# Routed tiles of a mixture of experts: five passes of TensorE for the second product in place of six, with the last 48 gated columns held twice

## What is computed

```
xn = layernorm(x)
attention: 16 heads of 128, keys and values from a latent of 128, causal softmax
moe:  scores = sigmoid(xn @ gate_w.T);  the two best of 8 experts, weights normalised, times 2.5
      h = einsum('td,edh->eth', xn, w1);  u = einsum('td,edh->eth', xn, w3)      # 176 hidden columns
      y = einsum('eth,ehd->etd', silu(h) * u, w2)
      routed = einsum('etd,te->td', y, combine)
      shared = silu(xn @ sw1) * (xn @ sw3) @ sw2
out = x + attention + routed + shared
```

## Time and profile before

| | before |
|---|---|
| median of 3 executions | 752.09 us |
| profiled execution, its own time | 751.67 us |
| its span, from the first to the last instruction | 749.9 us |
| mean granted clock of TensorE, as a share of full speed | 0.990 |
| busy share of the span: PE, VectorE, ScalarE, GpSimd | 94%, 86%, 78%, 66% |

### The profile page before, as it was taken

The page is one execution under the profiler, slowest core; times in us unless marked ns, Lnnn a source line. Parts: engine busy times, 40 slices in busy tenths (PEclk is TensorE's granted clock), DMA queues, the critical chain, the costliest instruction groups (busy, mean ns, idle before and its releaser), DMA issues.

```text
span 749.9 us, 15632 instructions
## 1 busy us (share of the span) xinstructions
PE 704.7 (94%) x4554; PEld 631.8 (84%) x4554; DVE 645.1 (86%) x1756; ACT 588.5 (78%) x1472; POOL 496.2 (66%) x450
## 2 busy tenths in 40 slices
PE   4788978999999999999999999999999999999975
PEld 3777767888888999999999999999999999987764
DVE  6577999999998888888888888988898889888886
ACT  3666667887878888888888888888988898887751
POOL 2544456778877677767876777677766767676620
PEclk9999999999999999999999999999999999999997
DMA  9553222543434444644464445544555454223201
GB/s 291 167 157 102 82 63 98 163 136 110 127 104 157 123 146 137 200 129 150 132 194 137 151 131 161 170 153 128 160 170 157 126 158 130 69 65 113 86 28 57
DMA packets 61396, 99.67 MB, mean 133 GB/s; under 512 B 9840, under 2 KB 33568, under 8 KB 61312
## 3 DMA queue, kind: packets, MB, share of 16 engines
q1 hardware_dynamic: 57904, 89.35, 39.2%
q0 software_dynamic: 3408, 9.33, 3.3%
HBM read 72.14 MB, written 26.51 MB: 132 GB/s over the span
## 4 chain that ended last, share of the span: by engine, by line
PE 68%; DVE 13%; POOL 6%; issue 5%; ACT 5%; DMA 1%; DVEq 0%; ACTq 0%; POOLq 0%
PE qk_proj L445 13%; PE u_acc L445 12%; PE scores L445 12%; PE out_acc L445 11%; PE ffn L445 10%; PE probs_t L548 6%; DVE acc L1235 2%; POOL swapped L910 2%; ACT swapped L760 1%; DVE rot L1181 1%; POOL rot L918 1%; POOL qk_lo L925 1%; DVE pt_lo L1212 1%; PE ffn L629 1%; POOL xs_sorted L941 1%
## 5 line engine op out<-in xcount | busy, mean ns | idle before, releaser
L910 POOL TENSOR_TENSOR swapped<-swapped,sin_t 128x512 f32<-128x512 f32 x128 | 164.9, 1288 | 180.3 <-DVE rot L1188 147.4
L925 POOL TENSOR_TENSOR qk_lo<-rot,qk_hi 128x512 fp32r<-128x512 f32 x128 | 163.3, 1294 | 11.2 <-ACT qk_hi L769 11.0
L780 ACT ACTIVATE probs<-scores,nbias 128x512 f32<-128x512 f32 (+3 forms) x256 | 134.9, 527 | 33.9 <-DVE nbias L1197 31.8
L1212 DVE TENSOR_TENSOR pt_lo<-probs_t,pt_hi 128x512 fp32r<-128x512 f32 x238 | 117.7, 495 | 48.0 <-ACT pt_hi L791 47.7
L760 ACT ACTIVATE swapped<-qk_proj 64x512 f32<-64x512 f32 x256 | 151.7, 592 | 6.2 <-PE qk_proj L445 1.6
L791 ACT ACTIVATE pt_hi<-probs_t 128x512 fp32r<-128x512 f32 x238 | 105.0, 441 | 44.6 <-PE probs_t L548 36.3
L1197 DVE CUSTOM_DVE_ANT_0 scores<-scores,mask 128x512 f32<-128x512 f32 (+3 forms) x256 | 125.3, 490 | 7.4 <-PE scores L445 1.6
L1235 DVE SCALAR_TENSOR_TENSOR acc<-out_acc,rsum,acc 128x256 f32<-128x256 f32 x256 | 111.0, 476 | 2.1
L548 PE MATMUL probs_t<-ident,probs 128*128 128x128 f32 x604 | 105.8, 274 | 7.4 <-DVE pt_lo L1212 6.8
L445 PE MATMUL scores<-qk_hi 128*128 128x512 f32 (+3 forms) x256 | 94.5, 369 | 3.5 <-ACT probs L780 3.2
L1181 DVE TENSOR_TENSOR rot<-qk_proj,cos_t 128x512 f32<-128x512 f32 x128 | 87.5, 684 | 10.1 <-ACT swapped L760 9.1
(11 more groups left out here) (182 smaller groups left out, 1837.6 us busy)
## 6 DMA issues: line engine op xcount, KB each, us to landing
wt<-expert_parts SPq DMA_DIRECT2D x39, 704.0 KB, 4.5
wt<-expert_parts SPq DMA_DIRECT2D x39, 512.0 KB
raw_a<-in_attn SPq DMA_DIRECT2D x8, 768.0 KB, 5.7
xs_sorted<-u_lo SPq DMA_DIRECT2D x3, 1670.5 KB, 9.1
xs<-xs_sorted SPq DMA_DIRECT2D x39, 128.5 KB, 2.9
expert_parts<-split SPq DMA_DIRECT2D x8, 352.0 KB, 2.3
expert_parts<-raw_f SPq DMA_DIRECT2D x8, 352.0 KB, 2.5
acc<-in_x SPq DMA_DIRECT2D x4, 512.0 KB, 6.7
```

Source lines behind the costliest of these rows:

```text
L780: ac.activation(probs[:, m % 2, PR_AT[i]:PR_AT[i] + n], s_bank[i % 2][:, 0:n], ACT.Exp, bias=nbias[:, m % 2, i:i + 1], scale=-1.0, accum_o ...
L910: pool.tensor_tensor(swapped[:, which, :], swapped[:, which, :], sin_t[:, :], ALU.mult).then_inc(sinm_ok[which], 1)
L925: pool.tensor_tensor(qk_lo[:, m % 2, which, :], rot[:, which, :], f32(qk_hi[:, m % 2, which, :]), ALU.subtract).then_inc(rlo_ok[which], 1)
L1212: ve.tensor_tensor(pt_lo[:, c], turn_bank(m, j)[:, 0:n], f32(pt_hi[:, c]), ALU.subtract).then_inc(ptlo_ok, 1)
```

## The change

For routed tiles alone, the 48 columns of the second chunk are held twice in `g`: in columns 128 to 175 and again in columns 192 to 239. Transposed, they stand in rows 0 to 47 and 64 to 111 of the second chunk. `g_hi` gets the rounded part in the lower half alone (rows 64 to 127), and zeros in the upper half, written once. The rest `g_lo`, which is the bank less `g_hi`, then holds the whole value (rounded as float32r) in rows 0 to 47 and the rest in rows 64 to 111. The weights of the second chunk are loaded twice too, to partitions 0 and 64. One pass of `g_lo` by the rounded weights gives hi by hi and lo by hi at once, and one pass of the 48 upper rows by the rests of the weights gives hi by lo. The shared expert's tiles keep six passes.

The diff, with the lines that only change blanks left out:

```diff
+REST, HALF = HID - P, P // 2
...
-            RAW_DMAS.append(RAW_DMAS[-1] + sum(len(cuts(e * HID + n, m, P)) for n, m in ((0, P), (P, HID - P))))
+            RAW_DMAS.append(RAW_DMAS[-1] + sum(n * len(cuts(e * HID + a, m, P)) for n, a, m in ((1, 0, P), (2, P, REST))))
...
-                        sp.dma_start(raw_f[a - first:z - first, W13 + c * D:W13 + c * D + D], src).then_inc(ld_raw, 16)
+                        for row in (0, HALF)[:c + 1]:
+                            sp.dma_start(raw_f[row + a - first:row + z - first, W13 + c * D:W13 + c * D + D],
+                                         src).then_inc(ld_raw, 16)
...
-                w = [(wt[:, 0, W13 + c * D:W13 + c * D + D], wt[:, 1, W13 + c * D:W13 + c * D + D]) for c in range(2)]
-                x = [(g_hi[:, c * P:c * P + P], g_lo[:, c * P:c * P + P]) for c in range(2)]
-                product(f_bank[:, 0:D], list(zip(x, w)), True, True).then_inc(y_ok, 1)
+                if t is None:
+                    w = [(wt[:, 0, W13 + c * D:W13 + c * D + D], wt[:, 1, W13 + c * D:W13 + c * D + D]) for c in range(2)]
+                    x = [(g_hi[:, c * P:c * P + P], g_lo[:, c * P:c * P + P]) for c in range(2)]
+                    product(f_bank[:, 0:D], list(zip(x, w)), True, True).then_inc(y_ok, 1)
+                    return
+                w = [wt[:, i, W13:W13 + D] for i in range(2)]
+                product(f_bank[:, 0:D], [((g_hi[:, 0:P], g_lo[:, 0:P]), w)], True, False)
+
+                w = [wt[:, i, W13 + D:FCOLS] for i in range(2)]
+                pe.matmul(f_bank[:, 0:D], g_lo[:, P:2 * P], w[0], start=False, stop=False)
+                pe.matmul(f_bank[:, 0:D], g_lo[0:REST, P:2 * P], w[1][0:REST, :], start=False, stop=True).then_inc(y_ok, 1)
...
-                ac.activation(g_hi[:, :], f_bank[:, 0:2 * P], ACT.Copy).then_inc(ghi_ok, 1)
+                if routed(f) is None:
+                    ac.activation(g_hi[:, :], f_bank[:, 0:2 * P], ACT.Copy).then_inc(ghi_ok, 1)
+                    return
+                if routed(f) == 0:
+                    ac.wait_ge(zero_ok, 4)
+                ac.activation(g_hi[:, 0:P], f_bank[:, 0:P], ACT.Copy)
+                ac.activation(g_hi[HALF:P, P:2 * P], f_bank[HALF:P, P:2 * P], ACT.Copy).then_inc(ghi_ok, 1)
...
+                if s == GAPS[-1]:
+
+                    pool.wait_ge(y_ok, STILES)
+                    pool.memset(g_hi[0:HALF, P:2 * P].bitcast(U32), 0).then_inc(zero_ok, 1)
...
-                ve.tensor_tensor(g[:, 0:HID], gated[:, :], f_bank[:, HID:UP], ALU.mult).then_inc(g_ok, 1)
+                last = ve.tensor_tensor(g[:, 0:HID], gated[:, :], f_bank[:, HID:UP], ALU.mult)
+
+                if routed(f) is not None:
+                    last = ve.tensor_tensor(g[:, P + HALF:P + HALF + REST], gated[:, P:HID],
+                                            f_bank[:, HID + P:UP], ALU.mult)
+                last.then_inc(g_ok, 1)
```

## The result

The changed kernel takes 758.94 us (median of four executions, 757.75 to 760.61), the kernel before, run beside it, 751.88 us. The ratio is 1.0105, with a 95% interval of 1.0082 to 1.0128: slower by 7.1 us, where 4.6 us less were forecast. The time lies inside the stated range of 746.4 to 762 us, but at its far end, where the rival of the emptying had put it (760.3 us).

The account below looks back on a forecast made before the run. TensorE was taken to bound the routed tiles; one pass fewer in 39 tiles saves 4.6 us and all other terms cost 0, giving 747.1 us, or 747.5 on the median. Range: 746.4 to 762 us.

Parts of the forecast that it names:

- the rival of the emptying: TensorE empties before and after the 48-row pass: +0.209 us a tile, +8.2, 760.3 us; chance 0.20.
- the price of the pass on 48 rows: Second chunk's last pass on TensorE: taken as 0.119 us, between bounds of 0.097 and 0.83.
- The first rival: TensorE empties around the 48-row pass, 0.164 us per change: 760.3 us, chance 0.20; weight load exposed too, 775.2 us, 0.12.
- the rival's dearer form: TensorE empties and the weight load is exposed too: +0.593 us a tile, +23.1, 775.2 us; chance 0.12.
- The bound: Routed tiles, 236.7 to 651.1 us: TensorE sets the steps, so one pass fewer saves 0.119 us in each of 39.
- The side work: VectorE's second write (0.20 us) and ScalarE's two copies (0.17 us more) a step: covered, no cost on the path.
- GpSimd's zeros: Written once on GpSimd, behind a wait for the last shared tile: cost nothing, at most 0.3 us once.
- the doubled loads: 48 more weight rows for each of 9 experts, 11 more SyncE issues: taken as nothing, 0.5 us as bound.
- One sign: VectorE's idle time ahead of pt_lo was to fall from 0.81 to about 0.6 us if the forecast was right.
- the 0.20 us: VectorE's second write, 48 more columns a step: delays its queue 0.20 us, absorbed in 0.81 us of idle time.
- The term of ScalarE: Two copies in place of one, 0.55 us for 0.38: 0.17 us more a step, no cost on the path.
- The cover: ScalarE's 0.40 us idle after rounding the keys fits the copies' 0.17 us; 0.23 us left, same in nearly all 39 steps.

Follow-up runs that it names:

- e3: The kernel before, with only the last of a routed tile's six passes on 48 rows: 764.52 us, ratio 1.0180.
- e5: The kernel before, with passes four and six of a routed tile on 48 rows and pass five on 128: 780.07 us, ratio 1.0381.
- e6: The changed kernel with its last pass on 112 rows instead of 48: 746.48 us, ratio 0.9930.
- e8: The changed kernel with its last pass on 32 rows instead of 48: 759.67 us, ratio 1.0126.
- e1: The changed kernel with its last pass on all 128 rows instead of 48: 745.88 us, ratio 0.9941.
- e7: e1 with five passes for the 16 shared tiles too and the zeros written at program start: 750.54 us, ratio 0.9991.
- e2: e1 with a sixth pass on 128 rows added, all extra copies, writes and loads kept: 750.57 us, ratio 1.0.
- e4: The kernel before, with the last three passes of a routed tile all on 48 rows: 763.0 us, ratio 1.0153.

## Why the prediction was wrong

**The step that failed** is the price of the pass on 48 rows, "I take 0.119, since it is nearest to the passes of the same 256 columns by the same 128 output rows". The passes of the same columns were the wrong neighbours. The number that decides is whether TensorE's next load may go ahead while the last pass runs, and no row of before could show it, since none had fewer than 128 rows. With the two changes that it brings, the pass cost 0.119 + 0.33 = 0.45 us, and not 0.119.

The first rival had the place and the sum: 2 x 0.164 - 0.119 = +0.209 us a tile, measured 10.755 - 10.543 = +0.212. That the two agree so closely is partly luck. Its 0.164 us a change was the duration of a pass less its distance to the next, and no change costs that: a change ahead of a pass costs 0.19 us and one ahead of the transposes 0.14 to 0.15, whose mean is 0.165 (e3, e5). Nor does the rival's dearer form hold, 0.164 and a whole weight load of 0.192 on top: what was measured is about the load alone. Its 760.3 us is 1.4 above the measured median; the routed stretch lost 8.3 us, where it said 8.2, and in the profiled pair the shorter tail hides part of that.

The Trainium skill, TensorEngine Tiling (Array Packing), Key Properties, says that a change of the tiling mode drains TensorE. It gives no price. The traces agree that a change costs, 0.33 us for a pair, but do not show how far TensorE drains. The Trainium skill, on the same page, Available Configurations, has tiles of 64 or 32 rows, and e6 (112 rows, no cost) and e8 (32 rows, the full cost) fit that, though no view names a mode and no run here tried 64 or 65 rows. What the Trainium skill, TensorE: Matmul & The Clock Gate, section LDWEIGHTS, says of the weight load nearly held, 183 ns for 48 rows against 192, but it answered another question than the one that mattered.

**What was right.** The bound: TensorE alone sets these steps, a pass is worth 0.119 us there (10.543 to 10.42 in e1), and it is worth nothing where other engines set the time (e7). The side work was covered, as e2 shows. GpSimd's zeros and the doubled loads did not appear. One sign did not come: VectorE's idle time ahead of pt_lo (128x384) was to fall from 0.81 to about 0.6 us and is still 0.81 in the changed kernel's plain step, and 0.80 on average in e1. Where the 0.20 us went was not followed.

**What was right only in part.** e1 saved 0.104 us a step on average and not 0.119: over 38 steps, from 241.91 to 646.94 us in the kernel before and from 241.25 to 642.33 in e1, the gain is 3.9 us where 4.5 was due. Five of the 38 steps, every eighth, are 10.51 us. (Five others are longer in every run, 11.42 us before and 11.31 to 11.34 in e1.) In the steps of 10.51 us ScalarE also rounds the next heads' weights, and it has no idle time left to hide the copies. Here is that step in the kernel before and in e1, ScalarE's timeline:

```profile
360.42 0.38 ACT L820 ACTIVATE g_hi<-ffn 128x256 fp32r<-128x256 f32 x1
360.69 0.63 ACT L769 ACTIVATE qk_hi<-rot 128x512 fp32r<-128x512 f32 x1
361.21 0.49 ACT L791 ACTIVATE pt_hi<-probs_t 128x384 fp32r<-128x384 f32 x1
361.72 0.59 ACT L760 ACTIVATE swapped<-qk_proj 64x512 f32<-64x512 f32 x1
```

```profile
358.56 0.28 ACT L837 ACTIVATE g_hi<-ffn 128x128 fp32r<-128x128 f32 x1
358.85 0.27 ACT L838 ACTIVATE g_hi<-ffn 64x128 fp32r<-64x128 f32 x1
359.15 0.63 ACT L781 ACTIVATE qk_hi<-rot 128x512 fp32r<-128x512 f32 x1
359.80 0.49 ACT L803 ACTIVATE pt_hi<-probs_t 128x384 fp32r<-128x384 f32 x1
360.32 0.59 ACT L772 ACTIVATE swapped<-qk_proj 64x512 f32<-64x512 f32 x1
```

From the start of g_hi to the start of pt_hi it was 0.79 us, and is 1.24. The durations say that 0.17 us more was added; the distances say 0.45. Before, g_hi, qk_hi and pt_hi each started 0.10 to 0.11 us ahead of the end of the one in front of it; in e1 the second copy, qk_hi and pt_hi start 0.01 to 0.03 us after it. The kernel before shows the pattern for two of them: of its 384 pairs of neighbouring instructions on ScalarE of which one works on 64 partitions, as swapped does, none overlaps, and of its 1084 pairs on 128 partitions 809 do. The second copy works on 64 partitions, so it lost the overlap on both of its sides: from the start of g_hi to that of qk_hi it is 0.26 us before and 0.59 in e1, in the plain steps too. The term of ScalarE is thus 0.32 us and not 0.17. Why pt_hi, two instructions further on, lost its overlap in these five steps is not shown. The cover was read from a step without the extra rounding, and the prediction took it to be the same in nearly all 39. Behind it VectorE's pt_lo ends at 360.89 and TensorE's load for the transposes comes at 360.94, where there were 0.50 us between them before:

```profile
360.33 0.56 DVE L1234 TENSOR_TENSOR pt_lo<-probs_t,pt_hi 128x384 fp32r<-128x384 f32 x1 [0.75 <-ACT pt_hi L803]
...
360.94 0.20 PEld L552 LDWEIGHTS probs_t<-ident,probs 128*128 128x128 f32 x2
```

That ScalarE alone is behind these 0.09 us was read from this timeline, and not tried by a run of its own.

## What to carry to other kernels

Where TensorE is the bound, a matmul cut to a few rows (48 or 32 here) between full ones is no saving, as the weight loads at both of its ends are no longer done ahead: pad it with rows of zeros or harmless terms (112 rows did as well as 128), or put all the narrow ones next to each other, so that the pair of changes is paid once (e4). Bound an operation that the trace does not show by what it might do to its neighbours' overlap (a pass's duration less its distance, or a weight load that is no longer hidden) before taking the price of the row that looks like it. And cost what is added to an engine's queue by distances from start to start, in the fullest step and not in a plain one.

## What the hardware showed that was not expected

- One narrow pass and three of them in a row cost the same, 0.33 us a tile (e3, e4); 32 rows cost as much as 48 (e8), and 112 cost nothing (e6).
- A change of the number of rows costs 0.19 us ahead of a pass and 0.14 to 0.15 ahead of transposes, close to the 0.18 and 0.14 us of the weight load that comes next (e3, e5).
- Splitting one ScalarE copy of 377 ns in two of 277 and 273, the second on 64 partitions, lengthened its queue by 0.32 us, and by 0.45 up to pt_hi in one step of eight, and not by 0.17. No instruction next to one on 64 partitions overlaps with it in the traces of before and e1 (in e7 two of 494 pairs do).
- The changed kernel's busy share of TensorE is the same 94% as before, and 100% in the stretch that lost 8.3 us.
